# Inverting the 8x8 diagonal blocks by substitution in a gated delta rule kernel

## The chip, the cores and the metric

One Trainium2 chip, one NeuronCore. The time is the device time of one execution in microseconds; the figure shown is the median of three runs. Engines go by their profile names: PE (TensorE), PEld (its weight loads), DVE (VectorE), ACT (ScalarE), POOL (GpSimd), SP (SyncE, which here only issues DMAs).

## The reference, cut to what matters

```
x: (4, 512, 256);  xn = layernorm(x)
attention branch (NV = 32 value heads, NK = 16 key heads, DK = DV = 128):
    mixed = silu(causal_conv4(xn @ W_qkv));  z = xn @ W_z
    beta = sigmoid(xn @ W_b);  g = -exp(A_log) * softplus(xn @ W_a + dt_bias)
    q, k, v = split(mixed);  q = l2norm(q) * DK**-0.5;  k = l2norm(k)
    for each token t:                       # per head, state S is 128 x 128
        S = S * exp(g_t)
        S = S + beta_t * k_t (v_t - k_t S)
        o_t = q_t S
    s = (rmsnorm(o) * norm_w * silu(z)) @ W_out
other branch: g = silu(mixture_of_experts(xn))
result: x + s * g
```

The kernel replaces the loop over tokens by chunks of C = 128 tokens. Within a chunk the tokens are coupled by a triangular 128 x 128 matrix B (products of keys, times decays and beta); the kernel needs the inverse of I + B. Everything is float32.

## The kernel before, in words

Three blocks follow each other: `prepare_block` (norms, small projections, decays), `ffn_block` (the other branch) and `recurrent_block`, in which nearly all the time goes and which alone is changed.

`recurrent_block` is a straight run of 64 steps (`STEPS`): 16 key heads (`i`), and for each the 4 sequences of the batch (`b`). A step handles U = 8 units: 2 value heads times 4 chunks. Each engine has its own hand written list of calls for a step, which it goes through in order; an instruction that waits for a semaphore holds back all that is listed behind it on its engine. The lists stand at L852 to L902 (PE), L1082 to L1119 (ACT), the end of the DVE section, and the end of the POOL section. Steps are pipelined. During step n the engines

- project, convolve and normalise q, k, v of step n: `project` (PE, L795), `first_tap` (ACT, L1033), `taps` (DVE, L1244, three per projection), `silu` (ACT, L1047), `by_token` (PE transposes, L812), `squares_by_token`, `k_beta`, `k_products`, `decayed_k`;
- invert the diagonal 32 x 32 blocks of B of step n (below);
- finish the inverse of step n-1 (`join_w`, `join_x` from 32 to 64, `halves_w`, `halves_x` from 64 to 128) and run its scan over the 4 chunks: `solve` (L682), `attend` (L692, L699), `new_state`, `read_state` (L667, L670), `residual`, `output`;
- gate, transpose and project out step n-2: `gating`, `gated_transpose`, `project_out` (L720), and compute z for step n-1: `project_z` (L728), `gate_z`.

The inversion before. `b_of_head` (DVE, L1272) writes B of all units; SP copies the four diagonal 32 x 32 blocks of each unit side by side into `bq` (128 partitions x 8 units x 32) with four DMAs (L628). POOL makes I minus the entries that couple neighbours (`pairs`), which is the inverse of the 2 x 2 blocks, and DVE transposes it within 32 x 32 blocks (`first_transpose`, L1291). Then four levels s = 2, 4, 8, 16 (`LEVELS`) double the block size each time. A level is a chain through four engines: POOL masks B (`mask_level`, L1446), PE multiplies (`merge_w`, L836), ACT copies with a minus sign (`take_merge`, L1079), PE multiplies (`merge_x`, L845), DVE adds and transposes (`merge`, L1296 and L1299). Each of `merge_w` and `merge_x` is 32 products of 32 x 32 (8 units, 4 blocks); a float32 product is two matmul instructions in the trace, so each shows as x64. At the end SP copies the result into `invT` and `inv` with six DMAs (L642, L644), for the next step's `halves`.

The log decays (`log_decays`, L1385, L1389, L1394) of step n+1 are made on POOL during step n from rows that a 1 MB DMA brings, and ACT takes their exponentials (`exp_decay`, L1005). Exp and SiLU need different tables on ACT, so a table load stands where they alternate.

Of the kernel before, what the change touches and what calls it, by code (L numbers as in the profile page):

```python
# [469 lines left out]
def recurrent_block(nc, x, w_in_dram, w_z_dram, w_out_dram, norm_dram, keep, g_rows, out):  # L470
# [10 lines left out]
    with ExitStack() as ctx:  # L481
# [176 lines left out]
        def _(pe):  # L658
# [898 lines left out]
```

## Time and profile before

| | |
|---|---|
| median of 3 runs | 3104.99 us (3104.87 to 3106.11) |
| the profiled execution: its time, its span | 3106.92 us, 3105.2 us |
| PE busy | 2854.6 us (92%) |
| PEld busy | 2109.6 us (68%) |
| DVE busy | 1899.5 us (61%) |
| ACT busy | 1661.2 us (53%) |
| POOL busy | 1147.7 us (37%) |
| mean granted TensorE clock | 0.975 |

Busy times overlap between engines and are shares of one span. The durations of matmuls in the timeline overlap their successors on PE, so what a group of them costs is read from the distance between its start and the next group's start. The profiled execution's time lies 1.9 us above the median of the runs and 1.7 us above its own span.

### The profile page before, as it was taken

The numbers are of one execution on the slowest core, as the hardware profiler recorded it, in microseconds if no ns is written. First come the engines' busy times: TensorE is split into PE (matmuls) and PEld (weight loads), VectorE is DVE, ScalarE is ACT, GpSimd is POOL, SyncE is SP. The second block draws the span as 40 slices with busy tenths as digits, with TensorE's granted clock in tenths as the row PEclk, the third lists the DMA queues.
The fourth block names the chain that finished last, engine by engine and source line by source line (L and its number), as shares of the span: only waits on it lengthen the run. The fifth ranks groups of instructions, "written<-read, shape, count | busy, mean of one in ns | idle before, by whom it ended". The sixth has DMA issues, their size and how long they took to land.

```text
span 3105.2 us, 120272 instructions
## 1 busy us (share of the span) xinstructions
PE 2854.6 (92%) x50586; PEld 2109.6 (68%) x50586; DVE 1899.5 (61%) x4174; ACT 1661.2 (53%) x5196; POOL 1147.7 (37%) x1519
## 2 busy tenths in 40 slices
PE   3399997999999999999999999999999999999995
PEld 2155555777776777777777777777777777777774
DVE  3223324667766677667676677766666666766663
ACT  2111112656665666656666566666666656665662
POOL 0222111444444444444444444444444444443441
PEclk9799998999999999999999999999999999999997
DMA  1522111111111111111111111111111111111111
GB/s 40 152 58 51 24 40 47 41 49 43 50 43 41 37 53 51 34 44 47 46 48 44 43 46 47 47 44 46 46 46 46 46 46 46 46 46 46 46 46 58
DMA packets 225770, 148.90 MB, mean 48 GB/s; under 512 B 187456, under 2 KB 195936, under 8 KB 225120
## 3 DMA queue, kind: packets, MB, share of 16 engines
q1 hardware_dynamic: 219104, 123.56, 13.9%
q0 software_dynamic: 6144, 17.83, 2.4%
q8 instruction: 395, 6.47, 0.9%
q14 instruction: 127, 1.04, 0.1%
HBM read 115.79 MB, written 2.70 MB: 38 GB/s over the span
## 4 chain that ended last, share of the span: by engine, by line
PE 61%; issue 10%; POOL 4%; ACT 3%; DVE 3%; DMA 1%; SPq 1%; POOLq 0%; DVEq 0%; ACTq 0%
PE rps L795 10%; PE rps L728 7%; PE rps L720 6%; PE rps L836 5%; PE rps L845 5%; PE rps L682 4%; PE rps L667 3%; PE rps L699 3%; PE rps L812 3%; PE rps L825 3%; PE rps L692 3%; PE rps L670 2%; PE rps L760 2%; PE rps L769 2%; PE rps L711 2%
## 5 line engine op out<-in xcount | busy, mean ns | idle before, releaser
L1244 DVE SCALAR_TENSOR_TENSOR conv<-rps,w_in,conv 128x509 f32<-128x509 f32 (+2 forms) x768 | 566.9, 745 | 23.3 <-ACT conv L1033 3.9
L795 PE MATMUL rps<-xnT,w_in 128*128 128x512 f32 x1024 | 498.9, 610 | 24.6 <-DVE cols L1226 13.2
L1420 POOL TENSOR_TENSOR decay_b<-decay,beta_k 128x512 f32<-128x512 f32 x128 | 130.4, 1040 | 783.5 <-DVE beta_k L1260 783.5
L947 ACT ACTIVATE upd<-rps 128x256 f32<-128x256 f32 x260 | 99.6, 383 | 423.3 <-PE rps L682 423.3
L720 PE MATMUL rps<-w_outn,gatedT 128*128 128x256 f32 x1056 | 295.8, 406 | 4.0 <-issue 3.1
L795 PEld LDWEIGHTS rps<-xnT,w_in 128*128 128x128 f32 x1024 | 175.3, 191 | 157.3 <-issue 125.2
L728 PE MATMUL rps<-w_z,xnT 128*128 128x256 f32 x1040 | 263.9, 387 | 2.0 <-ACT z L982 2.0
L845 PEld LDWEIGHTS rps<-xq,wq 32*32 32x32 f32 x16384 | 170.5, 105 | 135.7 <-issue 118.2
L1033 ACT ACTIVATE conv<-rps,w_in 128x512 f32<-128x512 f32 x256 | 175.6, 686 | 161.4 <-PE rps L795 161.2
L1296 DVE TENSOR_TENSOR xq<-rps,xq 128x256 f32<-128x256 f32 x256 | 108.7, 425 | 248.7 <-PE rps L845 247.7
L845 PE MATMUL rps<-xq,wq 32*32 32x32 f32 x16384 | 205.1, 194 | 56.9 <-issue 56.6
L836 PEld LDWEIGHTS rps<-xqT,bqs 32*32 32x32 f32 x16384 | 172.7, 107 | 98.4 <-issue 78.6
L836 PE MATMUL rps<-xqT,bqs 32*32 32x32 f32 x16384 | 202.7, 196 | 17.3 <-POOL bqs L1446 9.7
L436 DVE TENSOR_TENSOR silu_g<-fps_u,silu_g 128x512 f32<-128x512 f32 x68 | 47.0, 692 | 276.9 <-PE fps_u L455 128.7
L1079 ACT ACTIVATE wq<-rps 128x256 f32<-128x256 f32 x256 | 97.5, 381 | 208.3 <-PE rps L836 208.1
L720 PEld LDWEIGHTS rps<-w_outn,gatedT 128*128 128x128 f32 x1056 | 190.7, 201 | 25.6 <-issue 5.0
L728 PEld LDWEIGHTS rps<-w_z,xnT 128*128 128x128 f32 x1040 | 184.1, 192 | 29.9 <-issue 10.1
L1162 DVE SCALAR_TENSOR_TENSOR state<-state,cols,rps 128x128 f32<-128x128 f32 x260 | 78.7, 344 | 192.2 <-PE rps L692 191.9
L1152 DVE SCALAR_TENSOR_TENSOR resid<-rps,cols,v 128x128 f32<-128x128 f32 x390 | 116.2, 339 | 120.5 <-PE rps L667 120.5
L1446 POOL TENSOR_TENSOR bqs<-bq,cst 128x256 f32<-128x256 f32 x256 | 183.0, 725 | 0.0
L406 POOL DMA_DIRECT2D scale<-comb_rows x96 | 64.3, 701 | 314.1 <-DVE hid L439 223.2
L1070 ACT ACTIVATE v<-rps,k_norm 128x128 f32<-128x128 f32 x512 | 146.2, 376 | 58.4 <-PE rps L812 58.4
(208 smaller groups left out, 6450.3 us busy)
## 6 DMA issues: line engine op xcount, KB each, us to landing
sums_row<-g_rows SPq DMA_DIRECT2D x65, 1024.0 KB, 5.0
scale<-comb_rows POOLq DMA_DIRECT2D x40, 256.0 KB, 5.4
w_in<-in_w_in SPq DMA_DIRECT2D x17, 520.0 KB, 3.4
bq<-bmat SPq DMA_DIRECT2D x256, 32.0 KB, 2.0
inv<-xq SPq DMA_DIRECT2D x256, 32.0 KB
w_z<-in_w_z SPq DMA_DIRECT2D x17, 256.0 KB, 2.8
w_out<-in_w_out SPq DMA_DIRECT2D x17, 256.0 KB, 5.2
invT<-xqT SPq DMA_DIRECT2D x128, 32.0 KB
```

What stands on the lines that cost most here:

```text
L682: last = nc.tensor.matmul(ps[SCAN][:, g * P:(g + 1) * P], inv[r][:, g * NC_ + c, :], rhs, start=True, stop=True)
L720: last = nc.tensor.matmul(ps[OUT_BANK[c // 2]][:, (c % 2) * D:(c % 2 + 1) * D], gatedT[:, g, c * C:(c + 1) * C], w_outn[:, g, :], start=(g ...
L728: last = nc.tensor.matmul(ps[Z_BANK[c // 2]][:, (c % 2) * D:(c % 2 + 1) * D], xnT[:, m, tb * T + c * C:tb * T + (c + 1) * C], w_z[:, m, :] ...
L795: last = nc.tensor.matmul(ps[PROJ_BANK[j]][:, :], w_in[:, m * 4 * P + j * P:m * 4 * P + (j + 1) * P], xnT[:, m, b * T:(b + 1) * T], start= ...
L836: last = nc.tensor.matmul(ps[TRI][rows, u * Q:(u + 1) * Q], bqs[lv % 2][rows, u, :], xqT[rows, u, :], start=True, stop=True)
L845: last = nc.tensor.matmul(ps[TRI][rows, (U + u) * Q:(U + u + 1) * Q], wq[rows, u, :], xq[rows, u, :], start=True, stop=True)
L1033: nc.scalar.activation(conv[:, j, :], ps[PROJ_BANK[j]][:, :], ACT.Copy, scale=w_in[:, KT * 4 * P + j * KC + KC - 1:KT * 4 * P + (j + 1) * ...
L1070: last = nc.scalar.activation(v[p][:, j * NC_ + c, :], ps[TOK_BANK[2 + j]][:, c * C:(c + 1) * C], ACT.Copy, scale=k_norm[:, c:c + 1])
L1152: nc.vector.scalar_tensor_tensor(resid[:, g * P:(g + 1) * P], ps[SCAN][:, g * P:(g + 1) * P], col(k, NGAM, u), v[r][:, u, :], ALU.mult, AL ...
L1244: nc.vector.scalar_tensor_tensor(conv[:, j, shift:T], ps[PROJ_BANK[j]][:, 0:T - shift], w_in[:, k:k + 1], conv[:, j, shift:T], ALU.mult, A ...
L1420: nc.gpsimd.tensor_tensor(decay_b[:, us, :], decay[:, us, :], beta_k2[:, us].unsqueeze(2).to_broadcast([P, NC_, C]), ALU.mult).then_inc(db ...
L1446: return nc.gpsimd.tensor_tensor(dst[:, :, :], bq[:, :, :], cst[:, at:at + Q].unsqueeze(1).to_broadcast([P, U, Q]), ALU.mult)
```

## The change: substitution for the 8x8 blocks, two levels fewer, other lists

`LEVELS` becomes (8, 16). In place of `pairs` and levels 2 and 4:

- POOL masks `bq` to its 8 x 8 diagonal blocks (`blocks8`); DVE adds up the four groups of 8 columns (`compact`), of which one is not zero in a row, so that `b8` holds 8 entries per partition and unit;
- POOL spreads `b8` to `b8_rows`: seven copies, of which copy k is zero except on the partitions with p % 8 = k (`rows8`);
- one PE product with a 128 x 128 matrix of ones in 8 x 8 blocks (`spread_rows`) puts row k of each block on all 8 partitions of the block, for all units and k at once, 448 columns in PSUM;
- DVE runs the substitution (`substitute`): 13 dependent instructions on at most 56 elements per partition, then one that places the 8 x 8 results in `xq`, and the transposition.

```
@@ constants @@
-    parts = [r == c, r <= c, r > c, np.ones((P, P), bool), rq == cq, merge(1) * -1.0]
-    parts += [merge(s) for s in LEVELS]
+    parts = [r == c, r <= c, r > c, np.ones((P, P), bool), r // R == c // R]
+    parts += [rq // R == cq // R] + [merge(s) for s in LEVELS]
+    parts += [rq // R == cq[:, :G], r % R == cq[:, :R]]
@@ tensor @@
+    def spread_rows():
+        pe.wait_ge(x0_done, n(2) + 2)
+        pe.wait_ge(gT_done, n(2) + 1)
+        pe.wait_ge(x32_done, n(3) + 3)
+        nc.tensor.matmul(ps[TRI][:, 0:U * (R - 1) * R], cst[:, SAME8:SAME8 + P],
+                         b8_rows[:, :, :, :].rearrange("p u k j -> p (u k j)"), start=True, stop=True).then_inc(b8_ps, 1)
@@ vector @@
+    def compact():
+        dve.wait_ge(x0_done, n(2) + 1)
+        nc.vector.tensor_reduce(b8[:, :, :], bq8[:, :, :].rearrange("p u (q j) -> p u j q", q=G), AX.X, ALU.add).then_inc(b8_done, 1)
+    def substitute():
+        b_rows = ps[TRI][:, 0:U * (R - 1) * R].rearrange("p (u k j) -> p u k j", u=U, k=R - 1)
+        unit = cst[:, UNIT8:UNIT8 + R]
+        dve.wait_ge(b8_ps, n(1) + 1)
+        nc.vector.scalar_tensor_tensor(x8[:, :, 1:R], b_rows[:, :, 0, 1:R], neg_first[:, 0:1],
+                                       unit[:, 1:R].unsqueeze(1).to_broadcast([P, U, R - 1]), ALU.mult, ALU.add).then_inc(x8_done, 1)
+        for k in range(1, R - 1):
+            dve.wait_ge(x8_done, n(X8) + 2 * k - 1)
+            nc.vector.tensor_tensor(t8[:, :, k + 1:R], b_rows[:, :, k, k + 1:R],
+                                    x8[:, :, k:k + 1].to_broadcast([P, U, R - 1 - k]), ALU.mult).then_inc(x8_done, 1)
+            dve.wait_ge(x8_done, n(X8) + 2 * k)
+            nc.vector.tensor_tensor(x8[:, :, k + 1:R], x8[:, :, k + 1:R], t8[:, :, k + 1:R], ALU.subtract).then_inc(x8_done, 1)
+        ...
+        nc.vector.tensor_tensor(xq[:, :, :].rearrange("p u (q j) -> p u q j", q=G),
+                                x8[:, :, :].unsqueeze(2).to_broadcast([P, U, G, R]),
+                                cst[:, BLOCK8:BLOCK8 + G].unsqueeze(1).unsqueeze(3).to_broadcast([P, U, G, R]),
+                                ALU.mult).then_inc(x8_done, 1)
+        dve.wait_ge(x8_done, n(X8) + 2 * R - 2)
         nc.vector.transpose(xqT[:, :, :], xq[:, :, :]).then_inc(xqT_done, 1)
@@ gpsimd @@
-    def pairs():
+    def blocks8():
         pool.wait_ge(diag_in, i * (64 * BATCH) + 64 * (b + 1))
+        pool.wait_ge(b8_done, n(1))
+        masked(bq8, IN8).then_inc(x0_done, 1)
+    def rows8():
+        pool.wait_ge(b8_done, n(1) + 1)
+        pool.wait_ge(b8_ps, n(1))
+        nc.gpsimd.tensor_tensor(b8_rows[:, :, :, :], b8[:, :, :].unsqueeze(2).to_broadcast([P, U, R - 1, R]),
+                                cst[:, UNIT8:UNIT8 + R - 1].unsqueeze(1).unsqueeze(3).to_broadcast([P, U, R - 1, R]),
+                                ALU.mult).then_inc(x0_done, 1)
```

The four lists are also rewritten. In words, per engine: DVE runs `gating(1)`, `k_beta` earlier and later in the step than before (`k_beta` directly behind `taps(0)`), `decayed_k` later, and `compact` and `substitute` in the middle of the step. The two scan waits added (`gated_done` in `output(0)`, `q_pow` in POOL's `output_norms`) guard buffers. The places on which the prediction rests follow; names are those of the tiles (`rps` is a PSUM bank).

PE, the second half of a step, before, from the third level's first product on (L836 `merge_w`, L845 `merge_x`, L682 `solve`, L699 `attend`, L720 `project_out`, L812 `by_token`):

```order
L667 MATMUL rps<-state,qkT 128x256
L670 MATMUL rps<-state,qkT 128x256
L836 MATMUL rps<-xqT,bqs 32x32 x32
L682 MATMUL rps<-resid,inv 128x128 x2
L845 MATMUL rps<-xq,wq 32x32 x32
L699 MATMUL rps<-upd,scores 128x128 x2
L720 MATMUL rps<-w_outn,gatedT 128x256 x2
L836 MATMUL rps<-xqT,bqs 32x32 x32
L720 MATMUL rps<-w_outn,gatedT 128x256 x2
L845 MATMUL rps<-xq,wq 32x32 x32
L812 MATMUL rps<-cst,mixed 128x128 x4
```

The same half after, from the new product (L845 is now `spread_rows`, L854 `merge_w`, L863 `merge_x`, L732 `project_out`, L824 `by_token`, L740 `project_z`):

```order
L845 MATMUL rps<-b_rows,cst 128x448
L694 MATMUL rps<-resid,inv 128x128 x2
L732 MATMUL rps<-w_outn,gatedT 128x256 x6
L704 MATMUL rps<-upd,kw 128x128 x2
L711 MATMUL rps<-upd,scores 128x128 x2
L824 MATMUL rps<-cst,mixed 128x128 x4
L854 MATMUL rps<-xqT,bqs 32x32 x32
L679 MATMUL rps<-state,qkT 128x256
L682 MATMUL rps<-state,qkT 128x256
L863 MATMUL rps<-xq,wq 32x32 x32
```

Two of four levels are left, and between the new product and the first level stand a solve, three of the four output projections, an attend and a transposition.

PE, the first half of a step, before, behind `join_x` (L795 `project(2)`, L760 `halves_w`, L812 `by_token(1)`, L711 `gated_transpose`, L769 `halves_x`):

```order
L795 MATMUL rps<-xnT,w_in 128x512 x2
L760 MATMUL rps<-invT,bmat 64x64 x8
L812 MATMUL rps<-cst,qkT 128x128 x4
L711 MATMUL rps<-cst,gated 128x128 x4
L769 MATMUL rps<-inv,wh 64x64 x8
```

And after (L824 `by_token(1)`, L772 `halves_w`, L807 `project(2)`, L781 `halves_x`, L723 `gated_transpose`):

```order
L824 MATMUL rps<-cst,qkT 128x128 x4
L772 MATMUL rps<-invT,bmat 64x64 x8
L807 MATMUL rps<-xnT,w_in 128x512 x2
L781 MATMUL rps<-inv,wh 64x64 x8
L723 MATMUL rps<-cst,gated 128x128 x4
```

The transposition of k stands directly behind `join_x`, ahead of `project(2)`.

ACT before, the end of a step and the head of the next (L1005 `exp_decay`, L966 `squares`, L1079 `take_merge`, L1070 `take_v`, L1033 `first_tap`, L989 `take_join`, L1047 `silu(1)`):

```order
L1005 ACT_TABLE_LOAD
L1005 ACTIVATE decay<-log_d,cols 128x128 x4
L966 ACTIVATE gated,o_sq<-o 128x128 x2
L1079 ACTIVATE wq<-rps 128x256
L1005 ACTIVATE decay<-log_d,cols 128x128 x4
L1070 ACTIVATE v<-rps,k_norm 128x128 x4
L1033 ACTIVATE conv<-rps,w_in 128x512
L989 ACTIVATE wq<-rps 128x256
L1033 ACTIVATE conv<-rps,w_in 128x512
L1047 ACT_TABLE_LOAD
L1047 ACTIVATE qkT<-conv 128x512
```

ACT after, the middle of a step and what follows the exponentials (L1020 `exp_decay`, L969 `take_state_part`, L1075 `squares_by_token(0)`, L981 `squares`, L962 `take_updates`, L1062 `silu`):

```order
L1062 ACTIVATE mixed<-conv 128x512
L1020 ACT_TABLE_LOAD
L1020 ACTIVATE decay<-log_d,cols 128x128 x4
L969 ACTIVATE from_state<-rps,cols 128x128 x2
L1075 ACTIVATE conv,q_sq<-rps 128x128 x4
L981 ACTIVATE gated,o_sq<-o 128x128 x2
L962 ACTIVATE upd<-rps 128x256
L1020 ACTIVATE decay<-log_d,cols 128x128 x4
L1062 ACT_TABLE_LOAD
L1062 ACTIVATE mixed<-conv 128x512
```

Before, the exponentials closed the step, and the load of the SiLU table stood ahead of the next step's `silu(1)`; now both loads stand in the middle, and the next step starts with the SiLU table in place.

POOL before, from the decays by beta (L1420) over `pairs` (L1446, L1456), `k_norms` (L1427), two masks and `q_norms` (L1434 to L1442), behind which come one more mask and the log decays:

```order
L1420 TENSOR_TENSOR decay_b<-decay,beta_k 128x512 x2
L1446 TENSOR_TENSOR bq<-bq,cst 128x256
L1456 TENSOR_TENSOR xq<-bq,cst 128x256
L1427 TENSOR_TENSOR k_norm<-k_t,half 128x4
L1446 TENSOR_TENSOR bqs<-bq,cst 128x256 x2
L1434 TENSOR_TENSOR q_t<-q_sq,eps 128x4
```

POOL after, one step (L1459 decays by beta, L1424 to L1433 `log_decays`, L1485 `blocks8` and `mask_level`, L1498 `rows8`, L1466 `k_norms`):

```order
L1459 TENSOR_TENSOR decay_b<-decay,beta_k 128x512 x2
L1424 TENSOR_TENSOR log_d<-sums_row,cols 128x1024
L1428 AFFINE_SELECT log_d<-log_d 128x1024
L1433 TENSOR_TENSOR log_d<-log_d,sums_row 128x512 x2
L1485 TENSOR_TENSOR bq<-bq,cst 128x256
L1498 TENSOR_TENSOR b_rows<-b,cst 128x448
L1485 TENSOR_TENSOR bqs<-bq,cst 128x256
```

Before, the log decays stood behind the third mask; now they stand ahead of the first work on `bq`.

## Rows read from the trace of the kernel before

**Rows 1.** Windows view, one step: length, then PE, PEld, DVE, ACT, POOL; clock.
```profile
1548.50:1586.80 38.30, 37.65 (x770) 28.51 (x768) 27.53 (x64) 24.82 (x79) 16.69 (x22) 1.00 0.14 40
```

**Rows 2.** View of line L1256, once a step: durations in ns, first and last start.
```profile
L1256 DVE TENSOR_SCALAR k_t<-k_sq x64: 148/152/154, 533.4 to 3011.3; 128x4 f32<-128x4 f32 x64
```

**Rows 3.** Timeline of PE, end of a step: start, us, what, count.
```profile
1577.73 0.60 PE L670 MATMUL rps<-state,qkT 128*128 128x256 f32 x2
1578.36 0.74 PE L836 MATMUL rps<-xqT,bqs 32*32 32x32 f32 x64
...
1584.56 0.65 PE L812 MATMUL rps<-cst,mixed 128*128 128x128 f32 x4
1585.05 1.88 PE L795 MATMUL rps<-xnT,w_in 128*128 128x512 f32 x4
```

**Rows 4.** Timeline of PE, same step, where no 32x32 product stands between.
```profile
1560.06 1.88 PE L795 MATMUL rps<-xnT,w_in 128*128 128x512 f32 x4
1561.78 0.61 PE L692 MATMUL rps<-upd,kw 128*128 128x128 f32 x4
1562.23 0.61 PE L699 MATMUL rps<-upd,scores 128*128 128x128 f32 x4
1562.67 1.03 PE L720 MATMUL rps<-w_outn,gatedT 128*128 128x256 f32 x4
1563.54 0.59 PE L667 MATMUL rps<-state,qkT 128*128 128x256 f32 x2
```

**Rows 5.** Timeline of PE, same step, around the third projection; idle before in brackets.
```profile
1551.96 0.19 PE L751 MATMUL rps<-xq,wq 32*32 32x32 f32 x1
1552.68 1.98 PE L795 MATMUL rps<-xnT,w_in 128*128 128x512 f32 x4 [0.53 <-DVE conv L1244]
1554.59 1.14 PE L760 MATMUL rps<-invT,bmat 64*64 64x64 f32 x16
```

**Rows 6.** Timeline of PE in a longer step, two pieces of the merges.
```profile
988.65 0.32 PE L845 MATMUL rps<-xq,wq 32*32 32x32 f32 x13 [0.82 <-issue]
...
993.44 0.38 PE L845 MATMUL rps<-xq,wq 32*32 32x32 f32 x22 [1.48 <-issue]
```

**Rows 7.** The page's groups: count, busy us, mean ns, idle before and releaser.
```profile
L845 PE MATMUL rps<-xq,wq 32*32 32x32 f32 x16384 | 205.1, 194 | 56.9 <-issue 56.6
```

**Rows 8.** Timeline of ACT, head of the step of rows 5.
```profile
1551.56 0.69 ACT L1033 ACTIVATE conv<-rps,w_in 128x512 f32<-128x512 f32 x1 [1.52 <-PE rps L795]
1552.26 1.28 ACT L1047 ACT_TABLE_LOAD   x1
1553.56 0.63 ACT L1047 ACTIVATE qkT<-conv 128x512 f32<-128x512 f32 x1
```

**Rows 9.** Timeline of DVE, same step.
```profile
1546.72 0.42 DVE L1296 TENSOR_TENSOR xq<-rps,xq 128x256 f32<-128x256 f32 x1
1547.18 0.45 DVE L1299 STREAM_TRANSPOSE xqT<-xq 128x256 f32<-128x256 f32 x1
...
1550.31 2.31 DVE L1244 SCALAR_TENSOR_TENSOR conv<-rps,w_in,conv 128x509 f32<-128x509 f32 x3
...
1559.33 0.17 DVE L1260 TENSOR_TENSOR beta_k<-cols,k_inv 128x8 f32<-128x8 f32 x1
1559.53 0.17 DVE L1263 TENSOR_TENSOR wsuf_b<-beta_k,cols 128x8 f32<-128x8 f32 x1
...
1561.01 1.38 DVE L1272 TENSOR_TENSOR bmat<-rps,decay_b 128x512 f32<-128x512 f32 x2
```

**Rows 10.** Timeline of POOL, same step.
```profile
1559.58 2.04 POOL L1420 TENSOR_TENSOR decay_b<-decay,beta_k 128x512 f32<-128x512 f32 x2 [11.40 <-DVE beta_k L1260]
1566.36 0.74 POOL L1446 TENSOR_TENSOR bq<-bq,cst 128x256 f32<-128x256 f32 x1 [4.75 <-DMA bq<-bmat]
...
1574.87 1.89 POOL L1385 TENSOR_TENSOR log_d<-sums_row,cols 128x1024 f32<-128x1024 f32 x1
...
1578.17 2.49 POOL L1394 TENSOR_TENSOR log_d<-log_d,sums_row 128x512 f32<-128x512 f32 x2
```

More of the change, by code:

```diff
@@ L43 @@
 H = P // 2
-LEVELS = (2, 4, 8, 16)
+G = P // 4 // 8
+R = 8
+LEVELS = (8, 16)
 NL = len(LEVELS)
@@ L65 @@
 IDENT, UPTO, AFTER, ONES = (P * k for k in range(4))
-IDQ, MERGE1 = 4 * P, 4 * P + Q
-MERGE2 = MERGE1 + Q
-IOTA = MERGE2 + NL * Q
+SAME8, IN8 = 4 * P, 5 * P
+MERGE8 = IN8 + Q
+BLOCK8 = MERGE8 + NL * Q
+UNIT8 = BLOCK8 + G
+IOTA = UNIT8 + R
 NCONST = IOTA + E
@@ L855, in _ @@
                     join_x(n)
+                    by_token(1)
+                    halves_w(n)
                     project(2)
-                    halves_w(n)
-                    by_token(1)
+                    halves_x(n, r)
                     gated_transpose(n, 0)
-                    halves_x(n, r)
-                    pe.wait_ge(tap_done, n(12) + 6)
-                    gated_transpose(n, 1)
                     k_products(1)
@@ L865, in _ @@
                     solve(0)
-                    by_token(0)
                     project(3)
                     attend(0)
+                    pe.wait_ge(tap_done, n(12) + 6)
+                    gated_transpose(n, 1)
+                    read_state(1)
+                    by_token(0)
+                    solve(1)
+                    k_products(0)
+                    attend(1)
+                    pe.wait_ge(wz_in, (i + (1 if b == 0 else 2)) * 16)
+                    pe.wait_ge(tap_done, n(12) + 12)
+                    project_z(tb, 0)
+                    read_state(2)
+                    project_z(tb, 1)
+                    spread_rows()
+                    solve(2)
                     pe.wait_ge(ksq_done, n(1) + 1)
@@ L1301, in _ @@
                     gating(n, 0)
-                    gating(n, 1)
                     taps(1)
@@ L1305, in _ @@
                     taps(0)
+                    k_beta()
+                    gating(n, 1)
+                    halves(n, r)
                     taps(2)
-                    halves(n, r)
-                    k_beta()
-                    decayed_k(0)
-                    decayed_k(1)
                     b_of_head(0)
@@ L1316, in _ @@
                     taps(3)
-                    add_out(n, (b - 2) % BATCH, 0)
-                    first_transpose()
                     new_state(1)
                     output(1)
+                    compact()
                     residual(2)
-                    merge(0)
+                    decayed_k(0)
+                    decayed_k(1)
+                    substitute()
                     new_state(2)
                     output(2)
-                    merge(1)
-                    residual(3)
-                    scores_of_head(0)
-                    merge(2)
-                    output(3)
-                    scores_of_head(1)
-                    add_out(n, (b - 2) % BATCH, 1)
-                    merge(3)
+                    add_out(n, (b - 2) % BATCH, 0)
+                    residual(3)
+                    merge(0)
+                    scores_of_head(0)
+                    scores_of_head(1)
+                    output(3)
+                    add_out(n, (b - 2) % BATCH, 1)
+                    merge(1)
             n = counts(NK, 0)
```

109 lines of the change are left out of this document (48 added, 61 removed).

## The prediction, on record before the changed kernel ran

> **What bounds the kernel now.** First the busy shares, then the windows view of one step, then PE's timeline for that step, last the page's groups. In the step of [rows 1] the reader sees PE busy 37.65 of 38.30 us at full clock, against 27.53 for DVE, 24.82 for ACT and 16.69 for POOL: PE is the bound, and a step is as long as PE's list. From the start of `project(1)` at about 1547.1 to the next at 1585.05 [rows 3] it lasts 38.0 us. The mean step is longer: k_t comes once a step, 533.4 to 3011.3 in 63 intervals [rows 2], 39.33 us. In the longer steps PE stands still in the middle of a group of 32x32 products with nothing awaited, 0.82 and 1.48 us [rows 6]; `merge_x` alone has 56.6 us of this in all [rows 7]. So 39.33 = 38.0 + about 1.35 of such gaps and shorter disturbances. The 64 steps are 2517 of the 3105 us; what lies around them is not touched.
>
> **What goes on PE.** From L670 at 1577.73 to `project(1)` at 1585.05 [rows 3] are 7.32 us. They hold four of the eight halves of levels (two w, two x). Without them the rest would cost, at the undisturbed distances of [rows 4]: L670 half of an L720 (0.87, from 1562.67 to 1563.54), 0.43; one `solve` and one transposition like an L692, 0.45 each (1561.78 to 1562.23); L699 0.44; two L720, 1.74. Sum 3.51. The four halves with their waits and the slower neighbours are 7.32 - 3.51 = 3.8 us. The lists put the two remaining levels among the same kinds of work, so their cost stays. Also, before, `project(2)` waited 0.53 us [rows 5] for `taps(1)`; now `by_token(1)` and `halves_w` stand ahead of it and that wait has no place. Removed: 4.3 us.
>
> **What comes on PE.** One product of 448 columns. Four instructions of 512 take 1.72 us from start to start [rows 4], 0.43 each; two of 448 take 2 x 0.43 x 448/512 = 0.75 us. Lower bound 0.75, upper bound 0.87 (the L720 group). I take 0.75.
>
> **First new wait, `by_token(1)`.** It needs `silu(1)`. Let t = 0 at 1547.1. `join_x` starts its last product at 1551.96 [rows 5], so PE is free at 5.05. `first_tap(0)` on ACT starts at 1551.56, then comes the table load of 1.28 us, then `silu(1)`, 1553.56 to 1554.19 [rows 8]. In the new list SiLU is the last table used in the step before, so the load is not there: 4.5 + 0.69 = 5.15, plus 0.63, done at 5.8. `taps(1)` is no obstacle: with only four of the eight gating instructions ahead it ends at 4.9 (`project(1)` 1.8, a first tap 0.69 [rows 8] and a handoff of 0.1, then three taps in 2.31 [rows 9]). PE waits 5.05 to 5.9, 0.85 us. Behind it waits `halves_w`, and that also needs the six inverse DMAs, issued after the last transpose (1547.18 + 0.45 [rows 9]); they would be the later ones only if they took over 5.8 us. What this buys: the squares of k start at 6.4 and `k_beta` is done at 9.5, where wsuf_b was at 1559.7, 12.6 [rows 9]. But B is not made sooner, because `taps(2)` still stands ahead of `b_of_head`. DVE's new list, in t, with 2.31 for three taps, 1.38 for B [rows 9], 0.42 for a copy of 256 columns as in `merge` and 0.26 for each of 128: gating(0) 0.5 to 1.6; taps(1) 2.6 to 4.9; three join copies 5.1 to 6.4; taps(0) to 8.7; k_beta to 9.5; gating(1) to 10.6; halves to 11.3; taps(2) to 13.6; B to 15.0. Before it was 15.3 (1562.4).
>
> **Second new wait, `spread_rows`.** Chain: B done 15.0; four DMAs and their wait, 1562.39 to 1566.36 [rows 9, 10], 4.0, so 19.0. POOL is free by then: decays 9.4 to 11.4 (2.04), log decays from 1574.87 to 1578.17 + 2.49 = 5.8 us [rows 10], to 17.2. `blocks8` 0.74 [rows 10], 19.75. On DVE the walk goes on: new_state(0) and output(0) to 15.9; residual(1), after `read_state(1)`, 16.1 to 16.7; taps(3) to 19.0; new_state(1) and output(1) to 20.05; then `compact`. The reduction of 256 elements is not in the stretch; bounds are 0.17 (128x8) and 0.45 (128x256 transpose) [rows 9], I take the upper, it reads 256: 20.5. `rows8`, 448 elements on POOL, lies between 0.74 (256) and 1.02 (half of 2.04, for 512) [rows 10]; I take 1.0: 21.6. PE gets there as follows, with 0.45, 0.87 and 1.72 for four instructions of 128, 256 and 512 columns [rows 4], 1.91 for a projection beside small tiles and 1.14 for a halves group [rows 5]: `by_token(1)` 5.9 to 6.35; halves_w 7.45; project(2) 9.35; halves_x 10.45; gated_transpose 10.9; k_products(1), eight of 128, 11.8; solve 12.2; project(3) 13.95; attend 14.85; gated_transpose 15.3; read_state 16.15; transposition and solve 17.05; k_products(0) 17.9; attend 18.8; two project_z of 0.87 with a read_state between, 21.4. So the two meet; with the spread of the DMA chain I book 0.4 us.
>
> **The substitution.** 13 dependent instructions of 8 to 56 elements. Nearest rows: 128x8, started 0.20 apart (1559.33, 1559.53 [rows 9]). Farthest sensible row: a 128x256 that reads PSUM, 0.42, with a gap 0.46 [rows 9]. The mean width is about 30 elements, so I take 0.25: 3.25 us, bounds 2.6 and 6.0. Then xq 0.42 and the transposition 0.45, with gaps 4.2 us. PE meanwhile has a solve 0.45, three output projections like the L720 group, 2.6, attend 0.9, transposition 0.45 = 4.4 us [rows 4]: hidden, with 0.2 to spare. Behind `substitute` on DVE stand `new_state(2)`, `output(2)`, `residual(3)`; `read_state(3)` comes after `merge_w(0)` (0.7) on PE, so a `new_state(2)` of 0.6 is just in time. DVE gains 3.25 + 0.45 in a step and loses two levels, 2 x (0.46 + 0.45): 27.5 becomes 29.4 of 36, not a bound. ACT loses two copies. I book 0.4 for small collisions of these tight meetings: `take_updates(2)` behind the exponentials on ACT, `project_z(0)` behind `taps(3)`, `k_products(0)` behind `take_transposes(1)`.
>
> **The sum.** A step without gaps: 38.0 - 4.3 + 0.75 + 0.85 + 0.4 + 0.4 = 36.1. The gaps of 1.35: they sit in the 32x32 groups, of which two levels of four go; I take half, 0.65 off. Mean step 39.33 - 1.9 - 0.65 = 36.8; 64 x 2.55 = 163 us. The profiled execution took 3106.9 by its own time, so 2944 of that kind, and with the 1.9 by which it lay over the median, 2942.
>
> **Rivals.**
> (a) The gaps stay. They carry no releaser, so nothing in the profile ties them to the two levels. For: 1.48 us in one place. Against: fewer and less dense instructions. 64 x 1.9 = 122: 2983.
> (b) The meetings go well and all gaps vanish: the 0.4 and 0.4 are not paid. 64 x (1.9 + 0.8 + 1.35) = 259: 2846. For: the step of [rows 1] has no such gap, though it holds all four levels. Against: the DMA chain scatters.
> (c) DVE and POOL hold each other up. No row of before has a DVE instruction with two SBUF tensors beside a POOL instruction: the gating products run while POOL waits. In `substitute` six subtractions read two SBUF tensors while POOL does `mask_level(0)` and the norms, about 3.4 us of work. If each waits for a POOL instruction to end, the chain grows by some 2 us, of which 0.2 are covered: 2.55 - 1.8 = 0.75 a step, 48 us: 3057.
> The Trainium skill ("SBUF — State Buffer", Who interferes with whom) states this as a rule: a DVE instruction with two SBUF inputs contends with a GpSimd instruction that reads SBUF, and the later one blocks fully. By that rule the result is that of rival (c); no run so far shows it.
> (d) Slower: the substitution sets the step. Its 13 instructions hang on each other and PE has nothing beyond 4.4 us before `merge_w(0)`. Gain and slack are used up when 13 x (d - 0.25) = 2.55 + 0.2, at d = 0.46 us an instruction, just the 128x256 row. At 0.5 it is 13 x 0.25 - 0.2 - 2.55 = 0.5 a step, 32 us: 3137. Against: 128x8 rows at 0.17.
>
> **How the numbers follow.** Forecast 2942 with 0.52 (its own range 2905 to 2970), (a) 0.19, (b) 0.13, (c) 0.10, (d) 0.04, 0.02 for no change. Runs of this kernel agree within 0.05%; 0.2% is about what can be told. The range 2870 to 3020 holds the forecast, (a) and the nearer half of (b), leaving (c), (d) and the rest of (b) outside. Faster 0.94 (forecast, a, b, c), same 0.02, slower 0.04.
>
> **What would show it.** Windows of a step: PE busy about 34 of 36 to 37 us. Waits of PE: `by_token(1)` for ACT's `silu(1)`, about 0.85 a step; `spread_rows` for POOL under 1; `merge_w(0)` for DVE near zero. Substitution: 13 starts about 0.25 apart. If `merge_w(0)` waits over 1 us, (c) or (d) holds: by uneven distances (c), by even ones (d). If issue gaps per step are as before, (a). The forecast is wrong if the step without gaps is outside 35.3 to 36.8, or if PE waits elsewhere, for `take_updates` or `halves_w`, by more than 0.5 us.

## The result, and the profile after

The changed kernel took 3057.05 us (3046.75 to 3062.27) against 3104.93 for the kernel before on the same chip; the ratio is 0.9845, interval 0.9821 to 0.9869. It takes 1.5% less time, a difference clear of the noise, where 5.2% were forecast (3104.99 to 2942), and the measured time lies outside the range of 2870 to 3020. The mean step, read as in [rows 2] from k_t (now L1272, 527.8 to 2963.2), went from 39.33 to 38.66 us, where 36.8 were forecast.

| | before | after |
|---|---|---|
| median of runs | 3104.93 us | 3057.05 us |
| span of the profiled execution | 3105.2 us | 3060.6 us |
| PE busy | 2854.6 us (92%) | 2701.9 us (88%) |
| DVE busy | 1899.5 us (61%) | 2185.7 us (71%) |
| ACT, POOL busy | 1661.2, 1147.7 us | 1632.1, 1093.0 us |
| mean granted clock | 0.975 | 0.966 |

The window of one step of the kernel after, to set beside [rows 1] (length, then PE, PEld, DVE, ACT, POOL busy; clock):

```profile
1478.80:1516.68 37.88, 34.81 (x514) 26.45 (x515) 31.63 (x71) 22.82 (x69) 15.87 (x21) 1.00 0.16 46
```

PE has 2.8 us less to do in a step of nearly the same length: 3.1 us of this step it is not busy, against 0.65 before. The groups by line of the kernel after say where (count, busy us, mean ns, idle before and releaser):

```profile
L1204 DVE SCALAR_TENSOR_TENSOR gated<-o,o_r,z 128x128 f32<-128x128 f32 x528 | 339.9, 704 | 2.9 <-POOL o_r L1416 2.1
...
L863 PE MATMUL rps<-xq,wq 32*32 32x32 f32 x8192 | 100.1, 194 | 12.6 <-issue 12.4
...
L824 PE MATMUL rps<-cst,qkT 128*128 128x128 f32 x512 | 80.9, 281 | 43.6 <-ACT qkT L1062 43.6
```

The gating product of DVE, the same instruction on the same shape, now takes 704 ns on the average; before it was 353. `merge_x` (now L863) stands still for 12.6 us where it had 56.9 [rows 7]. The by_token(1) wait is 43.6 us, 0.68 a step. The largest wait of PE is not among these: L694, the first `solve`, has 119.4 us before it, 1.87 a step, all put down to "issue". The timelines of one step show it. DVE:

```profile
1492.74 1.09 DVE L1204 SCALAR_TENSOR_TENSOR gated<-o,o_r,z 128x128 f32<-128x128 f32 x4
...
1501.26 0.17 DVE L1276 TENSOR_TENSOR beta_k<-cols,k_inv 128x8 f32<-128x8 f32 x1
1501.46 0.17 DVE L1279 TENSOR_TENSOR wsuf_b<-beta_k,cols 128x8 f32<-128x8 f32 x1
1501.64 4.26 DVE L1204 SCALAR_TENSOR_TENSOR gated<-o,o_r,z 128x128 f32<-128x128 f32 x4
1505.83 0.67 DVE L1223 COPY inv<-rps 64x512 f32<-64x512 f32 x1
```

POOL, the same stretch (these answer to [rows 10]):

```profile
1501.50 2.08 POOL L1459 TENSOR_TENSOR decay_b<-decay,beta_k 128x512 f32<-128x512 f32 x2 [9.14 <-DVE beta_k L1276]
1503.55 1.94 POOL L1424 TENSOR_TENSOR log_d<-sums_row,cols 128x1024 f32<-128x1024 f32 x1
```

PE, the same stretch:

```profile
1503.17 1.06 PE L837 MATMUL rps<-qkT 128*128 128x128 f32 x8
1506.60 0.68 PE L694 MATMUL rps<-v,inv 128*128 128x128 f32 x4 [2.38 <-issue]
1507.12 1.88 PE L807 MATMUL rps<-xnT,w_in 128*128 128x512 f32 x4
...
1516.68 0.92 PE L845 MATMUL rps<-b_rows,cst 128*128 128x448 f32 x2
1517.44 0.61 PE L694 MATMUL rps<-resid,inv 128*128 128x128 f32 x4
```

The four products of gating(0) take 1.09 us, those of gating(1) 4.26. They start as `k_beta` ends, and that is what also starts POOL's two decays by beta; the first log decay follows at once. Taken one by one, the first product ends at 1502.69 (1501.64 + 1.05), POOL's first decay at 1502.54; the third starts at 1503.66 and ends at 1505.64, POOL's log decay at 1505.49; only the last, 0.34, is short. Behind the block stands the copy to `inv` (L1223), done at 1506.50, and PE's `solve(0)` starts at 1506.60. So "issue" here hides a wait for DVE: where that label carries 2 us at the same place in most steps, what stands on the other engines must be read by times.

The kernel after also holds the comparison within itself. In seven steps the block takes 2.62 us in place of 4.26, because POOL's log decay waits for its DMA and only the two decays stand beside the block. One of them, window (columns as above), DVE and POOL:

```profile
1000.80:1036.90 36.10, 34.19 (x514) 26.15 (x513) 29.87 (x72) 23.65 (x76) 15.90 (x20) 1.00 0.17 49
...
1001.73 2.63 DVE L1204 SCALAR_TENSOR_TENSOR gated<-o,o_r,z 128x128 f32<-128x128 f32 x4
...
1005.84 1.90 POOL L1424 TENSOR_TENSOR log_d<-sums_row,cols 128x1024 f32<-128x1024 f32 x1 [2.16 <-DMA sums_row<-g_rows]
```

PE waits 0.76 us ahead of `solve(0)` there, and that step takes 36.1 us, against 37.88 in the window above.

### The profile page after: what moved, and what is told of

It reads as the page before. It is cut to its first block, busy times and chain, and to the rows that moved or that the text cites. A ratio compares the mean times of both kernels' runs of the same rounds, so it can differ in the third digit from the quotient of the medians.

```text
span 3060.6 us, 88021 instructions
## 1 busy us (share of the span) xinstructions
PE 2701.9 (88%) x34330; PEld 1974.6 (65%) x34330; DVE 2185.7 (71%) x4880; ACT 1632.1 (53%) x5068; POOL 1093.0 (36%) x1391
## 4 chain that ended last, share of the span: by engine, by line
PE 63%; issue 12%; POOL 4%; DVE 3%; ACT 1%; POOLq 0%; DVEq 0%; ACTq 0%
PE rps L807 13%; PE rps L732 7%; PE rps L740 6%; PE rps L694 4%; PE rps L824 3%; PE rps L711 3%; PE rps L679 3%; PE rps L837 3%; PE rps L863 3%; PE rps L854 3%; PE rps L704 3%; PE rps L682 2%; PE rps L772 2%; PE rps L781 2%; PE rps L723 2%
## 5 line engine op out<-in xcount | busy, mean ns | idle before, releaser
L807 PE MATMUL rps<-xnT,w_in 128*128 128x512 f32 x1024 | 534.3, 647 | 13.5 <-DVE cols L1242 13.5
L1459 POOL TENSOR_TENSOR decay_b<-decay,beta_k 128x512 f32<-128x512 f32 x128 | 133.4, 1063 | 587.9 <-DVE beta_k L1276 587.9
L1204 DVE SCALAR_TENSOR_TENSOR gated<-o,o_r,z 128x128 f32<-128x128 f32 x528 | 339.9, 704 | 2.9 <-POOL o_r L1416 2.1
L962 ACT ACTIVATE upd<-rps 128x256 f32<-128x256 f32 x260 | 100.9, 388 | 381.4 <-PE rps L694 381.4
L807 PEld LDWEIGHTS rps<-xnT,w_in 128*128 128x128 f32 x1024 | 184.7, 201 | 155.8 <-issue 134.6
L740 PE MATMUL rps<-w_z,xnT 128*128 128x256 f32 x1040 | 279.2, 391 | 1.0 <-ACT z L997 0.7
L732 PE MATMUL rps<-w_outn,gatedT 128*128 128x256 f32 x1056 | 252.8, 383 | 1.0 <-ACT gatedT L991 0.7
L732 PEld LDWEIGHTS rps<-w_outn,gatedT 128*128 128x128 f32 x1056 | 192.4, 192 | 22.8 <-ACT gatedT L991 1.1
L740 PEld LDWEIGHTS rps<-w_z,xnT 128*128 128x128 f32 x1040 | 183.1, 191 | 22.2 <-ACT z L997 1.5
L981 ACT ACTIVATE gated<-o 128x128 f32<-128x128 f32 x520 | 156.7, 310 | 31.1 <-DVE o L1186 28.8
L1020 ACT ACTIVATE decay<-log_d,cols 128x128 f32<-128x128 f32 x520 | 167.0, 405 | 4.7 <-POOL log_d L1433 3.9
L1335 DVE TENSOR_TENSOR xq<-rps,xq 128x256 f32<-128x256 f32 x128 | 54.3, 424 | 160.7 <-PE rps L863 160.7
L460 PE MATMUL fps_g<-xnT,wg 128*128 x272 | 131.3, 606 | 41.0 <-DVE silu_g L441 28.7
L1433 POOL TENSOR_TENSOR log_d<-log_d,sums_row 128x512 f32<-128x512 f32 x130 | 162.6, 1271 | 5.4
L711 PE MATMUL rps<-upd,scores 128*128 128x128 f32 x1040 | 159.6, 276 | 0.0
```

The costliest lines, as they stand in the source:

```text
L711: last = nc.tensor.matmul(ps[OUT][:, g * P:(g + 1) * P], scores[r][:, g * NC_ + c, :], upd[:, g * P:(g + 1) * P], start=True, stop=True)
L732: last = nc.tensor.matmul(ps[OUT_BANK[c // 2]][:, (c % 2) * D:(c % 2 + 1) * D], gatedT[:, g, c * C:(c + 1) * C], w_outn[:, g, :], start=(g ...
L740: last = nc.tensor.matmul(ps[Z_BANK[c // 2]][:, (c % 2) * D:(c % 2 + 1) * D], xnT[:, m, tb * T + c * C:tb * T + (c + 1) * C], w_z[:, m, :] ...
L807: last = nc.tensor.matmul(ps[PROJ_BANK[j]][:, :], w_in[:, m * 4 * P + j * P:m * 4 * P + (j + 1) * P], xnT[:, m, b * T:(b + 1) * T], start= ...
L981: last = nc.scalar.activation(gated[:, c, g * P:(g + 1) * P], o[:, c, g * P:(g + 1) * P], ACT.Square, accum_out=o_sq[:, u:u + 1])
L1020: last = nc.scalar.activation(decay[:, u, :], log_d[:, u, :], ACT.Exp, bias=col(k, NLO, u))
```

## The experiments

Ratios are to the kernel before on the same chip, with their interval; that kernel's median was 3097 to 3105 us from one chip to the next, so differences of two medians below are good to some 10 us. The theory: POOL's running instruction holds a DVE product of two SBUF tensors until it ends, which lengthens the block of gating(1) by 3.2 us and moves the halves and so `solve(0)`. The rivals: the substitution is what limits the step, or the new lists do not give the gain even without either. The expectations of the runs call the theory P; D is that the DMAs that write SBUF at that time slow the products, L that DVE's list ahead of the halves is too long, whatever stands in it.

**e1: gating(1) ahead of k_beta**, nothing else changed:

```
-                    k_beta()
                     gating(n, 1)
+                    k_beta()
```

> The changed kernel with one call moved: VectorE runs gating(1) ahead of k_beta instead of behind it, so that it lies before GpSimd's decays by beta and log decays. Theory P (VectorE's product of two SBUF tensors, o and z, is held until GpSimd's running instruction, which reads SBUF, ends): the four products take 1.1 us together instead of 4.26, the wait of 2.4 us ahead of solve(0) on PE goes, time 3057 - 64 x 2.4 = 2903 (2880 to 2930). Theory D (the products are slow because six inverse DMAs and the 1 MB DMA of the row sums write SBUF at that time): they run at nearly the same time, so still 3.5 us or more, time 3040 to 3060. Theory L (VectorE's list ahead of halves is too long, whatever stands in it): same list length, 3050 to 3060.

Measured: 2893.13 us, 0.9356 [0.9326, 0.9386], against 0.9845 for the kernel after. The timeline of DVE, and the group by line:

```profile
1508.72 1.13 DVE L1204 SCALAR_TENSOR_TENSOR gated<-o,o_r,z 128x128 f32<-128x128 f32 x4
1509.77 0.17 DVE L1272 TENSOR_SCALAR k_t<-k_sq 128x4 f32<-128x4 f32 x1
...
1510.62 0.68 DVE L1223 COPY inv<-rps 64x512 f32<-64x512 f32 x1
...
L1204 DVE SCALAR_TENSOR_TENSOR gated<-o,o_r,z 128x128 f32<-128x128 f32 x528 | 150.7, 348 | 2.2 <-POOL o_r L1416 2.1
```

The block is back at 1.13 us, the group L1204 at 348 ns, and `solve(0)` has no wait. One swap of two calls is worth 164 us by the medians, 152 by the ratios. The profiled executions say how it divides. Their spans differ by 3060.6 - 2883.7 = 176.9 us, of which PE's idle time (the sum over all its groups) is 340.5 - 218.3 = 122. PE's busy time makes the other 55: by the mean clocks, 0.966 and 0.975, the time not granted is 104 and 72 us, so some 32 of the 55 are a lower clock; what makes the other 23 or so no run takes apart.

**e2: the second operand from PSUM.** gating(1) stays behind `k_beta`, beside POOL. z of the second value head is replaced by a PSUM bank in the steps 1 to 63, so its gate is left out of the result.

```
+                    other = ps[KK_BANK][:, c * P:(c + 1) * P] if g and 0 < n(1) - BASE < STEPS else z[:, c, part]
-                    ... o[:, c, part], o_r[:, u:u + 1], z[:, c, part], ...
+                    ... o[:, c, part], o_r[:, u:u + 1], other, ...
```

> The changed kernel with gating(1) where it is, but in steps 1 to 63 its second tensor is 128 columns of a PSUM bank in place of z (the gate z of the second head is left out), and k_products(1) waits for it. Theory P: one SBUF tensor only, nothing to hold it: the four take 1.1 to 1.5 us, the wait ahead of solve(0) goes, 2905 (2880 to 2935). Theories D and L: 3.5 us or more, 3040 to 3060.

Measured: 2891.97 us, 0.9331 [0.9304, 0.9358]. Groups by line:

```profile
L1206 DVE SCALAR_TENSOR_TENSOR gated<-o,o_r,z 128x128 f32<-128x128 f32 x276 | 82.7, 362 | 2.2 <-POOL o_r L1418 2.1
...
L1206 DVE SCALAR_TENSOR_TENSOR gated<-o,o_r,rps 128x128 f32<-128x128 f32 x252 | 70.9, 343 | 0.8
```

With one operand in PSUM the product takes 343 ns beside POOL's decays. It is the pair of SBUF operands beside POOL, not the place in the list, that costs.

**e4: POOL waits for gating(1)**, with DVE's list as in the kernel after:

```
+                    pool.wait_ge(gated_done, n(8) + 8)
                     decays_by_beta(0)
```

> The changed kernel, VectorE's list untouched; GpSimd waits for gating(1) before its decays by beta. Theory P: the four products take 1.1 us, the decays and log decays start 1 us later, which the DMA of the diagonal blocks covers: 2905 (2880 to 2935). Theory D: 3.5 us or more and everything on GpSimd later as well: 3060 or slower. Theory L: unchanged, 3050 to 3065.

Measured: 2896.21 us, 0.9349 [0.9317, 0.9381]; L1204 at 349 ns. Take POOL away, and the same product in the same place is short again; the later decays cost nothing that can be told from e1. Three ways of parting the two give the same time within their intervals, so the theory holds. Theories D and L fall: in e4 the DMAs and DVE's list are those of the kernel after, and the block is short. The rival of the lists falls too: they do give the gain.

**e3: the kernel before, with gating(1) behind k_beta**:

```
-                    gating(n, 1)     (ahead of taps(1))
                     ...
                     k_beta()
+                    gating(n, 1)
```

> The kernel before with one call moved: gating(1) behind k_beta, beside GpSimd's two decays by beta (1.04 us each), where it stood alone before. Theory P: the first two products last until the end of a GpSimd instruction each, the other two 0.3 us: 2.5 to 2.9 us in all; B is made some 1.5 us later, and of that PE loses up to 1.5 us a step: 3105 to 3200. Theory D: 1.1 us and 3095 to 3110.

Measured: 3511.77 us, 1.1318 [1.1281, 1.1355]: right on the block, but far above the expected 3105 to 3200. DVE:

```profile
1500.43 2.62 DVE L1190 SCALAR_TENSOR_TENSOR gated<-o,o_r,z 128x128 f32<-128x128 f32 x4
```

PE:

```profile
1503.20 1.09 PE L711 MATMUL rps<-cst,gated 128*128 128x128 f32 x4 [4.83 <-DVE gated L1190]
1504.09 1.92 PE L825 MATMUL rps<-qkT 128*128 128x128 f32 x8
1505.79 1.06 PE L682 MATMUL rps<-v,inv 128*128 128x128 f32 x4
...
1509.55 0.61 PE L692 MATMUL rps<-upd,kw 128*128 128x128 f32 x4
```

Here only the two decays stand beside the block, so it grows to 2.62 and not to 4.26. But the transposition that reads gating(1) stands early in PE's old list and waits 4.83 us (302.6 us in all), and behind the wait four products of 128 start 0.89 apart from the next group instead of 0.45 [rows 4]. The windows of PE (length, PE busy, clock) show the granted clock at half, the 1.2 GHz level; its mean over this kernel is 0.924:

```profile
1498.37:1503.20 4.83, 0.00 (x1) 0.81 0.00 0
1503.20:1506.60 3.40, 3.40 (x16) 0.50 0.00 0
```

**e10: e3 with PE's reader moved back.** `gated_transpose(1)` behind `attend(0)`, ACT's `take_transposes(1)` behind `first_tap(3)`, with a wait for `gated_done` in `output(0)` as guard.

```
+                    attend(0)
+                    pe.wait_ge(tap_done, n(12) + 6)
+                    gated_transpose(n, 1)
```

> e3_before_gating_behind with the second head's gated_transpose moved on PE behind attend(0), and its copy on ACT behind first_tap(3): PE no longer stands ahead of k_products and solve(0) for gating(1) (4.83 us a step in e3, followed by half clock). Theory: what made e3 slow was this wait, not the 1.5 us that the block costs VectorE: 3110 to 3200, products still 2.5 to 2.9 us together. If the block itself carries e3's time: over 3400.

Measured: 3231.06 us, 1.0414 [1.0393, 1.0435], clock 0.976, gating still 528 ns a product. Of e3's 414 us over the kernel before (3097.95 there), 281 were the wait on PE and the clock behind it. The expectation, 3110 to 3200, is missed by 31 us. The 132 left over the kernel before lie in scattered waits, the largest new one that of `project_out` for `gatedT`, 61.8 us, and of `merge_w` for POOL's masks, 32.4.

**e6: no substitution.** e1 without the 12 small instructions of the loop, so the 8 x 8 inverses are left out of the result.

```
-                        for k in range(1, R - 1):
-                            ... two tensor_tensor ...
+                        dve.sem_inc(x8_done, 2 * R - 4)
```

> e1_gating_ahead with the 12 small instructions of the substitution's loop left out (the first one, the placing and the transposition stay), so 2.7 us less on VectorE. Theory H (the loop is hidden behind PE's work between spread_rows and merge_w(0)): the same time as e1, 2893 within 10. Theory V (VectorE paces the step): up to 64 x 2.7 = 170 us less, 2720 to 2800.

Measured: 2867.08 us, 0.9272 [0.9237, 0.9307]. 26 us, 0.4 a step, for a loop of some 2.7 us. Theory H allowed 10 us and is missed by 16, so the loop is nearly hidden and not wholly; theory V (2720 to 2800) is far off. The rival of the substitution falls as the cause of the lost time.

**e7: twice the substitution.** e1 with 12 more small products, each behind the last, that write a tile nobody reads later.

```
+                        for k in range(1, R - 1):
+                            for half in range(2):
+                                ... tensor_tensor(t8[:, :, k + 1:R], ...) ...
```

> e1_gating_ahead with 12 more small dependent products of the same sizes in the substitution, on the tile t8 only (the result stays): 2.7 us more on VectorE between the loop and the placing. In e1 the transposition ended at 1526.53 and merge_w(0) began at 1526.89, 0.36 us of slack, so theory H expects 64 x (2.7 - 0.4) = 147 us more, 3040 (3000 to 3060), with PE waiting ahead of merge_w(0). If the time moves by less than 60, later work gives it back.

Measured: 3190.18 us, 1.0304 [1.0281, 1.0327], a miss: 130 us above the upper end of what was expected. PE:

```profile
1528.86 1.08 PE L855 MATMUL rps<-xqT,bqs 32*32 32x32 f32 x64 [3.14 <-DVE xqT L1337]
1529.87 1.22 PE L680 MATMUL rps<-state,qkT 128*128 128x256 f32 x2
```

PE waits 204.3 us in all for `xqT`, 3.2 a step at this place, but the time grew by 297: the matmuls behind the wait run at the lower level (granted clock 0.50 in the 3.4 us behind it; L680's two of 256 columns take 1.01 us to the next start, four such 0.87 in [rows 4]), and the mean clock falls from 0.975 to 0.932. The slack of the substitution is small, as rival (d) said; the substitution as written just fits into it.

**e5: only fewer levels.** The kernel before in its old lists, `LEVELS = (2, 4)`, the calls of levels 2 and 3 dropped on all engines. The blocks are joined only up to 8 x 8, so the inverse is incomplete.

```
-LEVELS = (2, 4, 8, 16)
+LEVELS = (2, 4)
-                    merge_w(2)   merge_x(2)   merge_w(3)   merge_x(3)   (and their partners)
```

> The kernel before with LEVELS = (2, 4): the calls of the third and fourth level are left out on all engines (the inverse is not complete), nothing put in their place, no call moved. It prices what is removed. The prediction's sum: 3.8 us a step on PE and half of the gaps of 1.35 us: 3107 - 64 x 4.45 = 2822. If the gaps stay (theory G1): 2865. If they fall to a third, as in the changed kernel, where idle time of the 32x32 products fell from 74 to 14 us in all (theory G2): 2795 to 2815.

Measured: 3054.62 us, 0.9846 [0.9801, 0.9891]; a gain of only 1.5%, a miss. Groups by line:

```profile
L795 PE MATMUL rps<-xnT,w_in 128*128 128x512 f32 x1024 | 523.9, 636 | 153.2 <-DVE conv L1238 112.4 <-DVE acc L1190 27.6 <-DVE cols L1220 13.2
L699 PE MATMUL rps<-upd,scores 128*128 128x128 f32 x1040 | 165.1, 281 | 30.3 <-ACT upd L943 30.3
L682 PE MATMUL rps<-resid,inv 128*128 128x128 f32 x780 | 132.3, 292 | 28.6 <-DVE resid L1146 28.6
...
L1184 DVE SCALAR_TENSOR_TENSOR gated<-o,o_r,z 128x128 f32<-128x128 f32 x528 | 149.2, 355 | 163.4 <-POOL o_r L1369 163.4
```

Without the two levels PE waits 112.4 us at `project(2)` for taps(1), 10.0 before. taps(1) stands behind all eight gating products, and these wait 163.4 us for POOL's output norms, 12.8 before. In the old lists the levels had filled that time. Removed work on the bound was turned into a wait.

**e9: the old algorithm in new lists.** `pairs` and four levels, put into the lists of e8 (below).

```
-LEVELS = (8, 16)
+LEVELS = (2, 4, 8, 16)
-                    spread_rows()
+                    merge_w(0)
-                    substitute()
+                    merge(0)          (levels 1 to 3 among project_out and project_z)
```

> The lists of e8_project_first with the old algorithm: pairs and four levels in place of the 8x8 substitution, and no product for the rows. It prices the algorithm alone, in lists that do not run into the block of VectorE. The prediction's terms: 3.8 - 0.75 = 3.05 us a step more on PE than e8, 64 x 3.05 = 195, 3049; with the gaps of before on top (about 1 us a step) up to 3113. If the new lists alone made e8's gain (rival), it would be 2854 to 2900.

Measured: 3152.92 us, 1.0166 [1.0149, 1.0183], a miss: 40 us above the upper end of 3113. PE waits 67.0 us for `resid` (0.8 before) and stands still for 48.6 in `merge_x` with nothing awaited. Against e8 the algorithm is worth 299 us in these lists, where 195 to 259 were expected; the new lists alone bring nothing to the old one.

**e8: project(2) first.** e1, and PE's first half as: `project(2)` between `join_x` and `by_token(1)`, `gated_transpose(0)` ahead of `halves_x`.

```
+                    project(2)
                     by_token(1)
                     halves_w(n)
-                    project(2)
-                    halves_x(n, r)
                     gated_transpose(n, 0)
+                    halves_x(n, r)
```

> e1_gating_ahead with PE's list changed in one place: behind join_x come project(2), by_token(1), halves_w, gated_transpose(0), halves_x. The 0.67 us that PE waited for silu(1) are filled by project(2), which waits for taps(1) only (0.1). halves_x then waits up to 0.3 for ACT's take_halves. Expected gain 0.4 to 0.5 us a step, 25 to 32 us: 2863 (2855 to 2875). If k_beta comes later than gating(1) ends (it stood at 8.7 us in the step, the squares of k will be done at about 8.8), the decays and B move by 0.1 only; if more hangs on it, no gain: 2890.

Measured: 2853.88 us, 0.9218 [0.92, 0.9235], just under the expected 2855 to 2875. It is the best version, 203 us ahead of the kernel after (194 by the ratios). Groups by line:

```profile
L824 PE MATMUL rps<-cst,qkT 128*128 128x128 f32 x512 | 77.3, 274 | 0.0
L781 PE MATMUL rps<-inv,wh 64*64 64x64 f32 x1040 | 75.0, 223 | 11.8 <-ACT wh L1011 11.3
```

The by_token(1) wait of 43.6 us is gone, at the price of 11.3 at `halves_x`; 39 us came back.

**e11: PE's order of e8 in the kernel after**, gating(1) left where it is. The edit is that of e8 on PE alone.

> The changed kernel with only PE's list of e8 (project(2) ahead of by_token(1)); VectorE's gating(1) stays behind k_beta and is blocked. If VectorE's path gating(1), halves, solve(0) sets the step, the filled wait of 0.67 us on PE turns up in the wait ahead of solve(0): 3050 to 3065. If PE's list sets it: 3057 - 64 x 0.5 = 3025.

Measured: 3112.02 us, 1.0037 [1.0009, 1.0065], a miss: the order that gains 39 us in e1 loses 55 here. PE:

```profile
1518.80 1.16 PE L837 MATMUL rps<-qkT 128*128 128x128 f32 x8
1522.85 1.19 PE L694 MATMUL rps<-v,inv 128*128 128x128 f32 x4 [2.89 <-issue]
1523.84 3.62 PE L807 MATMUL rps<-xnT,w_in 128*128 128x512 f32 x4
```

PE arrives sooner at the same late `solve(0)` and waits 2.89 instead of 2.38 us (168.3 in all, against 119.4), and then runs the third projection in 3.41 us to the next start instead of 1.72. Its windows beside those of the kernel after (first e11, then after):

```profile
1519.96:1522.85 2.89, 0.00 (x1) 0.88 0.00 0
1522.85:1526.25 3.40, 3.40 (x7) 0.50 0.02 5
```

```profile
1504.20:1506.60 2.40, 0.03 (x1) 1.00 0.00 0
1506.60:1510.00 3.40, 3.40 (x19) 1.00 0.00 0
```

Clock times span gives the time not granted: 155 us, against 104 in the kernel after. The 51 between them account for the loss of the whole execution (3108.8 - 3060.6 = 48): PE's busy time grew by 43.5 us, 2701.9 to 2745.4, and its idle time hardly, since the by_token(1) wait went as the other grew.

## Why the prediction was wrong, point by point

The step that failed is in the walk of DVE's list: "gating(1) to 10.6", with 1.1 us for its four products. They took 4.26. The walk had the products start at 9.5, and it had POOL's decays start at 9.4; the two numbers stood a few lines apart and were not put together. With 3.2 us more the walk's own numbers give the wait: halves at 14.5 in place of 11.3, PE ready at 11.8, so 2.7 us. Measured, `solve(0)` waits 2.38 us (1.87 on the mean) where nothing was booked, and the clock takes a part more. Undoing just this (e1) moved the kernel by 164 us.

- Rival (c) named the cause and put it in the wrong place. Its 3057 us agree with the result by accident: they were worked out for the subtractions in `substitute`.
- The ground of rival (c), that no row of before has such a pair, and "no run so far shows it", were wrong for the trace as a whole. The rows came from steps in the middle. Ahead of the first step of the kernel before, the eight gating products meet the log decays:

```profile
511.85 6.90 DVE L1190 SCALAR_TENSOR_TENSOR gated<-o,o_r,z 128x128 f32<-128x128 f32 x8
...
511.90 1.89 POOL L1385 TENSOR_TENSOR log_d<-sums_row,cols 128x1024 f32<-128x1024 f32 x1 [7.45 <-DVE cols L1226]
```

  Eight products take 6.90 us where twice 1.1 were usual; the first takes 2.09 and ends 0.15 behind POOL's. The price of the pair stood in the trace before the change.
- The Trainium skill ("SBUF — State Buffer", Who interferes with whom) says that the later of the two instructions blocks fully. The traces agree at gating(1), where products of 0.35 us last until POOL's running instruction ends (1.98 us for the third), and e2 and e4 take the effect away from either side. Which came first is not sharp: the first product at 511.85 started 0.05 us ahead of POOL by the record and was held all the same. In `substitute` the effect is small: the last subtraction, 128x8, takes 235 ns on the mean, and the product of the same width that reads PSUM 172. The timeline of DVE after has one step's loop, and ahead of it the last subtraction of the step before:

```profile
1482.55 0.50 DVE L1321 TENSOR_TENSOR x<-x,t 128x8 f32<-128x8 f32 x1
...
1514.69 0.61 DVE L1307 TENSOR_REDUCE b<-bq 128x64 f32<-128x256 f32 x1
...
1517.64 0.27 DVE L1314 SCALAR_TENSOR_TENSOR x<-rps,neg_first,cst 128x56 f32<-128x56 f32 x1 [0.24 <-PE rps L845]
1517.95 0.21 DVE L1318 TENSOR_TENSOR t<-rps,x 128x48 f32<-128x48 f32 x1
1518.19 0.21 DVE L1321 TENSOR_TENSOR x<-x,t 128x48 f32<-128x48 f32 x1
...
1520.41 0.17 DVE L1321 TENSOR_TENSOR x<-x,t 128x8 f32<-128x8 f32 x1
1520.62 0.43 DVE L1325 TENSOR_TENSOR xq<-x,cst 128x256 f32<-128x256 f32 x1
```

  And POOL beside that subtraction:

```profile
1481.30 1.02 POOL L1466 TENSOR_TENSOR k_norm<-k_t,half 128x4 f32<-128x4 f32 x1
1482.30 0.72 POOL L1485 TENSOR_TENSOR bqs<-bq,cst 128x256 f32<-128x256 f32 x1
```

  It takes 0.50 instead of 0.17 and ends at 1483.05, as POOL's mask does at 1483.02. Beside `k_norm`, 1.02 us long on 128x4, the subtractions before it were not held up: not every POOL instruction with SBUF operands holds DVE up. There the trace does not agree with the rule, and what decides stays open. In the whole step shown the 13 starts lie 0.21 to 0.31 apart, 2.98 us from the first to the placing of the result; 3.25 were booked.
- The terms of the sum, with what the kernel after and e1 measured. Product of 448 columns: 0.75 booked, 0.76 measured (1516.68 to 1517.44). Wait of by_token(1): 0.85 and 0.68. Wait of `spread_rows`: 0.4 booked; 8.6 us in all, 0.13 a step, in the kernel after and 5.3, 0.08, in e1. Small collisions: 0.4 and about 0.05 (`project_z`, `project_out` and the later solves, 3.6 us in all in e1). `halves_w`, for which nothing was booked: 17.8 us in all, 0.28 a step, and 0.24 in e1, against 0.10 before. `rows8` 1.0 and 0.96; `compact` 0.45 and 0.61. `project(2)` no longer waits, as said.
- With the block out of the way the forecast was on the safe side: e1's mean step is 35.94 us (k_t, 528.9 to 2793.1), 0.9 below the 36.8, and the waits booked and not paid are (0.85 + 0.4 + 0.4) - (0.68 + 0.08 + 0.05) = 0.84. That the two agree so well is partly luck, for more of the gaps went than was booked (next point) and `halves_w` cost more. e1 lies inside the range that was given for the change.
- Of the issue gaps "half" was taken to go. `merge_x` had 56.9 us in all and has 12.6 now, 16.2 in e1, so more went. With `merge_w` the groups had 74.2 us and have 17.4 in e1: 0.89 a step gone, where 0.65 were booked. Why PE stands still in these groups stays open; no run here takes the gaps apart.
- The sign that was announced for (c), a wait of `merge_w(0)` over 1 us at uneven distances, did not show: 1.4 us in all. The text did look elsewhere on PE ("if PE waits elsewhere"), for `take_updates` and `halves_w`, but not for `solve(0)`. The general sign did show: the step of the window above, 37.88 us, lies outside 35.3 to 36.8.

## What to carry to other kernels

When calls move in a list, write down for every DVE instruction with two SBUF inputs what POOL runs at that moment, above all where one event releases both: here `k_beta` started both the product and its obstacle. Put such a product ahead of the event, or give it a PSUM operand. Before saying that a trace holds no such meeting, look for the longest instance of the instruction in the whole trace, its start included. Work taken off the bound is a gain only if the lists are rewritten with it (e5 against e1), and an order of PE is good or bad together with its latest input (e8 against e11).

## What the runs showed of the hardware that was not expected

- Several POOL instructions in a row hold several DVE products in a row: with two decays (e3) four products take 2.62 us, with two decays and the log decay behind them 4.26, alone 1.09 to 1.14.
- A mean clock hides what a wait does. In the steps shown, the groups behind PE waits of 2.89, 3.14 and 4.83 us (e11, e7, e3) ran at the 1.2 GHz level, and those behind one of 2.38 in the kernel after did not (1.88 us for the next projection). Over all steps it is a matter of how often: the 3.4 us behind the wait had a lowered clock in 16 of 50 steps of the kernel after (waits of 1.73 to 2.48 us), in 46 of 54 of e11 (2.52 to 2.89), in 56 of 63 of e7 (3.08 to 3.62) and in 63 of 63 of e3 (4.19 to 4.83). What the lower level cost came on top: 297 us for 204 us of wait in e7. In each of the three cases the expectation had priced only the wait.
